# Edge tiles gathered once into a ring addressed through registers, in a graph-attention and mixture-of-experts kernel

## The reference

```python
xh = (x @ W).reshape(N, H, D)                    # H = 8 heads, D = 32
a_src = jnp.einsum('nhd,hd->nh', xh, att_src)
a_dst = jnp.einsum('nhd,hd->nh', xh, att_dst)
e = jax.nn.leaky_relu(a_src[src] + a_dst[dst], NEG_SLOPE)
m = jax.ops.segment_max(e, dst, num_segments=N)
e = jnp.exp(e - m[dst])
denom = jax.ops.segment_sum(e, dst, num_segments=N)
alpha = e / denom[dst]
msg = xh[src] * alpha[:, :, None]
out = jax.ops.segment_sum(msg, dst, num_segments=N).reshape(N, H * D) + bias
```

## Time and profile before

| what | value |
|---|---|
| time, median of 3 runs | 1908.13 us (1907.54 to 1909.66) |
| profiled execution | 1906.79 us, of which the span from first to last instruction is 1904.5 us |
| granted TensorE clock, mean | 0.952 |
| edge stage on DVE, first score to last add | 105.5 to 1200.0 us, 110 batches |
| busy over the whole span: PE, DVE, ACT, POOL | 89%, 74%, 58%, 64% |

### The profile page before, as it was taken

The page is one execution under the profiler, slowest core; times in us unless marked ns, Lnnn a source line. Parts: engine busy times, 40 slices in busy tenths (PEclk is TensorE's granted clock), DMA queues, the critical chain, the costliest instruction groups (busy, mean ns, idle before and its releaser), DMA issues. The chain is left out here.

```text
span 1904.5 us, 37710 instructions
## 1 busy us (share of the span) xinstructions
PE 1688.9 (89%) x10846; PEld 1183.9 (62%) x10846; DVE 1402.6 (74%) x3850; ACT 1106.3 (58%) x2386; POOL 1212.2 (64%) x1141
## 2 busy tenths in 40 slices
PE   6679889899898988989989798837999999999997
PEld 5445455455554645545555454625898898898995
DVE  6787778778687876887868778996666666666664
ACT  3556667667676666775767665773434434434343
POOL 1377777777777777777777777202566665665653
PEclk9889989989899998998999999977999999999999
DMA  8654555555555555545555453592333233333322
GB/s 282 215 147 123 143 167 145 137 154 143 167 145 134 156 142 167 146 132 155 145 167 145 127 139 104 218 351 77 48 52 52 47 53 51 48 53 49 49 44 32
DMA packets 124146, 240.41 MB, mean 126 GB/s; under 512 B 25064, under 2 KB 82996, under 8 KB 122772
## 3 DMA queue, kind: packets, MB, share of 16 engines
q0 software_dynamic: 62800, 147.76, 32.9%
q1 hardware_dynamic: 51816, 80.51, 12.9%
q10 hardware_dynamic: 9340, 9.73, 1.5%
HBM read 195.47 MB, written 43.30 MB: 125 GB/s over the span
## 5 line engine op out<-in xcount | busy, mean ns | idle before, releaser
L1142 POOL DMA_INDIRECT gather_ring<-node_table,src_slot x879 | 836.8, 952 | 270.6 <-issue 254.1
L1270 PE MATMUL bank<-gather_ring,onehot 128*128 128x264 f32 x1758 | 563.4, 403 | 51.1 <-DVE gather_ring L1194 50.3
L1236 PE MATMUL bank<-ones 128*128 128x512 bf16 x1787 | 558.0, 392 | 51.3 <-ACT gather_ring L1312 39.7
L1270 PEld LDWEIGHTS bank<-gather_ring,onehot 128*128 128x128 f32 x1758 | 293.8, 194 | 259.7 <-DVE gather_ring L1194 214.7
L1166 DVE TENSOR_TENSOR acc<-acc,bank 128x264 f32 x879 | 371.5, 423 | 14.1 <-PE bank L1270 13.1
L1194 DVE TENSOR_TENSOR gather_ring<-gather_ring,bank 128x256 f32<-128x256 f32 x879 | 363.3, 414 | 0.3 <-ACT bank L1311 0.3
L2164 POOL DMA_INDIRECT out_rows<-y,token_idx x105 | 202.7, 1930 | 218.1 <-DMA out_rows<-y,token_idx 155.7
L2133 ACT ACTIVATE hid<-bank,cols 128x256 f32<-128x256 f32 (+1 forms) x448 | 209.9, 550 | 148.5 <-PE bank L2074 145.6
L1236 PEld LDWEIGHTS bank<-ones 128*128 128x128 bf16 x1787 | 171.1, 100 | 199.5 <-issue 80.1
L2074 PE MATMUL bank<-xe,w_hi 128*128 128x256 f16 (+1 forms) x1792 | 285.3, 268 | 1.7 <-DVE xe L1996 1.5
L2091 PE MATMUL bank<-w,hid_hi 128*128 x1680 | 278.4, 273 | 0.0
(11 more groups left out here) (320 smaller groups left out, 1999.1 us busy)
## 6 DMA issues: line engine op xcount, KB each, us to landing
stage<-in_L_ffn_W SPq DMA_DIRECT2D x16, 1024.0 KB
dst_row<-dst_rows SPq DMA_DIRECT2D x110, 128.0 KB, 3.5
gather_ring<-node_table,src_slot POOLq DMA_INDIRECT x879
w_split<-w_out SPq DMA_DIRECT2D x32, 256.0 KB, 3.1
w<-w_split SPq DMA_DIRECT2D x8, 1024.0 KB, 9.8
node_table<-acc ACTq DMA_DIRECT2D x24, 264.0 KB
r_ring<-in_x_lanes SPq DMA_DIRECT2D x7, 896.0 KB, 8.1
xt<-in_x_lanes SPq DMA_DIRECT2D x24, 256.0 KB, 4.7
```

What stands on the lines that cost most here:

```text
L1142: e.indirect_dma_start(out=gather_ring[:, b % GB, j, :], out_offset=None, in_=node_table, in_offset=bass.IndirectOffsetOnAxis(ap=src_slot[ ...
L1236: e.matmul(to[:, :].rearrange("p (k n) -> p k n", k=2), halves[:, 0:P], halves.rearrange("p (a n) -> p a n", a=1).broadcast_to([P, 2, 2 * ...
L1270: e.matmul(bank[AGG[s % len(AGG)]][:, 0:ROW], onehot[:, b % OHB, j, :], gather_ring[:, b % GB, j, :], start=True, stop=True).then_inc(summ ...
```

## The change

Five edits that belong together:

- POOL gathers each **edge tile** once (832 indirect DMAs in 104 batches, the last tile padded) instead of each slot (879 in 110). `src_tile` takes the place of `src_slot`, and is made directly by loading `src_pad` and turning it, so that of the 14 indirect gathers of stage 1 seven are left.
- A slot no longer has a fixed place in `gather_ring`. Each slot's place (0 to 31) is worked out in stage 1 into `slot_table` and read into registers (`load_places`); the score and the message address the ring through them. `load_tiles` moves from before the score to after the second slot of the batch ahead; `load_places` stands after its sixth slot.
- Since rows are read by place, the score's first operation (128x64 for eight slots) becomes eight of 128x8.
- Since a tile may be read by two slots, a message can't overwrite its row: it goes to `message_ring` of 12 slots, from which PE reads; ACT writes the exponentials there. POOL waits for `messages`, up to a count read from `slot_table` (`SPANS_AT`, one register load for 8 batches).
- Which landing a batch of slots needs is known only on the chip. SP waits for it (`landed`, with counts in registers, loaded every other batch) and passes it on to DVE as `rows_landed`. The `onehot` ring shrinks from 3 to 2.

```diff
-        src_slot = early.take("src_slot", [P, SLOTS_UP], I32)
+        src_tile = early.take("src_tile", [P, ceil_div(ET, EB) * EB], I32)
...
+        MR = 12
+        message_ring = early.take("message_ring", [P, MR, ROW])
+        OHB = 2
...
+                    e.dma_start(raw_src[:, :, :], src_pad.rearrange("(c t) p -> t c p", t=P)).then_inc(src_loaded, 16)
...
+                e.tensor_copy(slot_table[SPANS_AT:SPANS_AT + 32, 0:SLOT_GROUPS * PER_GROUP],
+                              bank[7][SPANS_AT:SPANS_AT + 32, P:P + SLOT_GROUPS * PER_GROUP]).then_inc(slot_keys_made, 1)
+                for h in range(2):
+                    hs = slice(h * HALF_SLOTS, (h + 1) * HALF_SLOTS)
+                    vector_order.of(e.tensor_copy(slot_table[PLACES_AT:P, hs], bank[5 + h][PLACES_AT:P, 0:HALF_SLOTS]))
...
+                e.tensor_single_scalar(slot_table[PLACES_AT:LANDED_AT, :], slot_table[PLACES_AT:LANDED_AT, :], PLACES - 1,
+                                       ALU.bitwise_and).then_inc(slot_keys_made, 1)
...
+            if n == SRC_AT - 1:
+                e.wait_ge(src_loaded, 16)
+                e.tensor_copy(raw_src_f[:, :, :], raw_src[:, :, :]).then_inc(src_cast, 1)
...
+        def load_row_of(e, row, at, n, least, most):
+            _, values = nc.values_load_multi_w_load_instructions(
+                slot_table[row:row + 1, at:at + n], engines=[e.engine], min_val=least, max_val=most,
+                skip_runtime_bounds_check_because=IN_RANGE)
+            return values
...
         def pool_edges(e, batches):
-            for b in batches:
-                if b >= GB:
-                    e.wait_ge(summed, (b - GB + 1) * EB)
-                for j, s in enumerate(slots_in(b)):
+            for t in batches:
+                if t >= GB:
+                    if (t - GB) % SPANS_AT_ONCE == 0:
+                        at = t - GB
+                        spans = load_row_of(e, SPANS_AT, at, min(SPANS_AT_ONCE, TILE_BATCHES - GB - at), 1, USED)
+                    e.wait_ge(messages, spans[(t - GB) % SPANS_AT_ONCE])
+                    e.sem_inc(m_sems["passed"], 1)
+                for j, i in enumerate(tiles_of(t)):
                     e.indirect_dma_start(
-                        out=gather_ring[:, b % GB, j, :], out_offset=None, in_=node_table,
-                        in_offset=bass.IndirectOffsetOnAxis(ap=src_slot[:, s:s + 1], axis=0)
-                    ).then_inc(gathered[b % GB], 16)
+                        out=gather_ring[:, t % GB, j, :], out_offset=None, in_=node_table,
+                        in_offset=bass.IndirectOffsetOnAxis(ap=src_tile[:, i:i + 1], axis=0)
+                    ).then_inc(gathered[t % GB], 16)
...
             def score(b):
-                e.wait_ge(gathered[b % GB], 16 * (EB * (b // GB) + len(slots_in(b))))
+                e.wait_ge(rows_landed, GB * (b + 1))
...
-                vector_order.of(e.tensor_tensor(zbuf[:, 0, :, :], gather_ring[:, b % GB, :, D:ROW],
-                                                picked[:, b % 2, :, 0:HEADS], ALU.add))
+                for j in range(len(slots_in(b))):
+                    vector_order.of(e.tensor_tensor(zbuf[:, 0, j:j + 1, :], row_at(b, j)[:, :, D:ROW],
+                                                    picked[:, b % 2, j:j + 1, 0:HEADS], ALU.add))
...
+                if s >= MR:
+                    e.wait_ge(summed, s - MR + 1)
+                e.tensor_tensor(message_ring[:, s % MR, 0:D].rearrange("p (h d) -> p h d", d=DH),
+                                row_at(b, j)[:, :, 0:D].rearrange("p a (h d) -> p (a h) d", d=DH),
...
+                    if j == 1 and b + 1 < BATCHES:
+                        load_tiles(e, b + 1)
                     if j == EB // 2 - 1:
                         vector_weights_between(e, b)
+                    if j == EB - 3 and b + 1 < BATCHES:
+                        load_places(e, b + 1)
...
+            load_tiles(e, 0)
+            load_places(e, 0)
             sum_picks(0)
             for b in range(BATCHES):
-                load_tiles(e, b)
                 score(b)
...
+            def landed(b):
+                if b % 2 == 0 and b >= GB:
+                    values = load_row_of(e, LANDED_AT, b * GB, min(2, BATCHES - b) * GB, 16 * EB,
+                                         16 * EB * ceil_div(TILE_BATCHES, GB))
+                    landed_regs[b], landed_regs[b + 1] = values[0:GB], values[GB:]
+                for q in range(GB):
+                    if b >= GB:
+                        e.wait_ge(gathered[q], landed_regs[b][q])
+                    elif q <= b:
+                        e.wait_ge(gathered[q], 16 * EB)
+                    e.sem_inc(rows_landed, 1)
```

More of the change, by code:

```diff
@@ L186, in build_gnn_moe @@
         s1 = Region(early_b)
+        TILES_AT, SPANS_AT, PLACES_AT, LANDED_AT = 0, 32, 64, 96
+        PLACES = GB * EB
+        TILE_BATCHES = ceil_div(ET, EB)
+        assert PLACES & (PLACES - 1) == 0 and GB * BATCHES <= SLOTS_UP and SLOTS_UP // EB >= TILE_BATCHES
         iota_slot = s1.take("iota_slot", [P, SLOTS_UP])
         above = s1.take("above", [P, SLOTS_UP])
+        raw_src = s1.take("raw_src", [P, SLOT_GROUPS, P], I32)
+        raw_src_f = s1.take("raw_src_f", [P, SLOT_GROUPS, P])
         raw_idx = s1.take("raw_idx", [P, 4, P], I32)
@@ L236, in build_gnn_moe @@
         slot_base = s1w.take("slot_base", [P, SLOT_GROUPS])
+        PER_GROUP = P // EB
+        batch_end = s1w.take("batch_end", [P, PER_GROUP])
+        is_end = s1w.take("is_end", [P, PER_GROUP])
+        end_keys = s1w.take("end_keys", [P, SLOT_GROUPS, PER_GROUP])
+        last_batch = s1w.take("last_batch", [P, BATCHES], I32)
         pad_src = s1w.take("pad_src", [P, P], I32)
@@ L547, in vector_slot_step @@
                 e.tensor_scalar(above[:, :], iota_slot[:, :], key[:, 0:1], None, ALU.is_gt).then_inc(slots_counted, 1)
+                e.wait_ge(pool_const, BATCH_END)
+                vector_order.of(e.tensor_scalar(is_end[:, :], batch_end[:, :], part[:, 0:1], None, ALU.is_equal))
+                e.wait_ge(vector_order.sem, vector_order.n)
+                e.scalar_tensor_tensor(end_keys[:, :, :], key[:, :].rearrange("p (g a) -> p g a", a=1).broadcast_to(
+                    [P, SLOT_GROUPS, PER_GROUP]), 1.0, is_end[:, :].rearrange("p (a j) -> p a j", a=1).broadcast_to(
+                    [P, SLOT_GROUPS, PER_GROUP]), ALU.add, ALU.mult).then_inc(slots_counted, 1)
             elif 0 < c < SLOT_GROUPS:
-                e.wait_ge(slots_counted, c)
+                e.wait_ge(slots_counted, c + 1)
                 e.scalar_tensor_tensor(above[:, :], iota_slot[:, :], key[:, c:c + 1], above[:, :], ALU.is_gt, ALU.add
@@ new lines, in vector_slot_step @@
+            thresholds = slot_table[landed, 0:BATCHES * GB].rearrange("p (b q) -> p b q", q=GB)
+            if n == LISTS_AT + 5 + SLOT_GROUPS:
+                e.wait_ge(vector_order.sem, vector_order.n)
+                for q in range(GB):
+                    vector_order.of(e.tensor_single_scalar(thresholds[:, :, q], last_batch[landed, :], GB - q, ALU.add))
+                e.wait_ge(vector_order.sem, vector_order.n)
+                vector_order.of(e.tensor_single_scalar(thresholds, thresholds, 2, ALU.arith_shift_right))
@@ new lines, in vector_slot_step @@
+            g = n - LISTS_AT - 15
+            if 0 <= g < SLOT_GROUPS:
+                end = min((g + 1) * P, SLOTS)
+                e.wait_ge(slots_turned, g + 1)
+                e.tensor_single_scalar(neg_dst[:, g * P:end], bank[SLOT_TURN[g % 2]][:, 0:end - g * P], -1.0, ALU.mult
+                                       ).then_inc(slots_kept, 1)
+                e.wait_ge(slots_based, g + 1)
+                vector_order.of(e.tensor_scalar(row_up[:, :], raw_f[:, g % 2, :], 1.0, 0.0, ALU.add, ALU.max))
+                e.wait_ge(vector_order.sem, vector_order.n)
+                e.tensor_single_scalar(raw_row[:, g, :], row_up[:, :], float(P + 1), ALU.min
+                                       ).then_inc(rows_clamped, 1)
@@ L1295, in make_onehot, with ring_parts @@
                 one_where_zero(onehot[:, b % OHB, :, :], made, onehot_made)
+            def ring_parts(b):
+                first = min(EB, MR - b * EB % MR)
+                return [(0, first)] + [(first, EB - first)] * (first < EB)
             e.wait_ge(vector_const, MINUS_ONE_UP)
@@ L1311, in scalar_edges @@
                 e.activation(weights(b), zbuf[:, 1, :, :], ACT.Exp).then_inc(weighed, 1)
-                e.activation(gather_ring[:, b % GB, :, D:ROW], zbuf[:, 1, :, :], ACT.Exp).then_inc(weighed, 1)
+                if b:
+                    e.wait_ge(summed, (b + 1) * EB - MR)
+                for j, n in ring_parts(b):
+                    at = (b * EB + j) % MR
+                    made = e.activation(message_ring[:, at:at + n, D:ROW], zbuf[:, 1, j:j + n, :], ACT.Exp)
+                made.then_inc(weighed, 1)
                 if b + 2 < BATCHES:
@@ L1326, in load_row @@
```

(8 more changed lines are left out.)

148 lines of the change are left out of this document (83 added, 65 removed).

## The result

The changed kernel takes 1962.93 us (median of 4 runs, 1962.46 to 1967.12) against 1907.92 of the kernel before on the same chip: ratio 1.0297, 95% interval 1.0285 to 1.0309. The forecast was 1916 us with a range from 1874 to 1943. The sign is right, +55 us where +8 were forecast, and the time lies outside the range.

A forecast was written before the change was run, and what follows sets the result against it. POOL's issue rate bounds the edge stage before, DVE after: 110 x 1.23 = +135.3, less 144.8 of gather waits, +14 W1 blocks, +1.1 first loads, +3 stage 1 = +8.6 us; forecast 1916 us, range 1874 to 1943.

The forecast's parts named there:

- What bounds, and what POOL gives back: Edge stage: POOL's issue rate bounds before, DVE after; 47 fewer gathers free 59.1 us of POOL; DVE's 144.8 us wait goes.
- The rival in which POOL stays the bound: Edge stage: mid-batch loads covered and score pairs cheap, so DVE needs 8.75 us a batch; about 1855 us; chance 0.05.
- the one of SP's late landings: SP passes landings on late between stores and loads; at most some 0.5 us in each of eight batches; no chance given.
- Step 1, the joined score: DVE's score: eight 128x8 operations behind register instructions, 0.125 us a pair, replace one 128x64; +0.82 us a batch.
- The rival of cheap scores: DVE's score: register instruction and operation overlap, 0.08 us a pair; 35 us less in all, 1882 us; chance 0.22.
- Step 2, the register loads: DVE's batch: two mid-batch loads at 0.39 to 0.40 us each replace one at the turn (0.39); +0.41 us a batch.
- Step 3, the message's register instruction: DVE's messages: each one's own register instruction, 0.057 us, is hidden behind the running add, so it adds nothing.
- The rival of the lost cover: DVE's messages: the new register instruction lengthens each slot by 0.03 us, 26 us, 1942 us; chance 0.17 together with a dearer pair.
- The W1 blocks: Eight batches where DVE waits for picks behind a block's load: saved gather wait partly returns, mean 1.8 us each, +14 us.
- Start and stage 1: First two loads ahead of the first picks and score, +1.1 us; DVE's small work in stage 1, +3 us (0 to +6).

The follow-up runs named there:

- The fastest version: Changed kernel, both tables in words on partition 0, places loaded right behind the sum of the picks, tiles behind mid-batch W1 work: 1901.7 us, ratio 0.9957.
- four kernels above: Changed kernel, both loads at the turn: 2352.1 us; kernel before with two turn loads: 2187.2; second from partition 64: 1906.9; score in eight without registers: 1907.9.

## Why the prediction was wrong, step by step

- **What bounds, and what POOL gives back:** right. DVE is the bound, POOL's wait for the messages is 103.4 us (forecast +40; it is larger by about what DVE became slower), the gathers are as short as before, and DVE's 144.8 us of waiting are gone. The rival in which POOL stays the bound falls by this, and the one of SP's late landings too: DVE waits for no landing of rows in this trace.
- **Step 1, the joined score, +0.82 us:** right. 1.08 - 0.26 = 0.82 in the batch shown, 0.85 in the mean over the batches. The pair that I took at 0.125 us averages 0.129. The rival of cheap scores falls: 0.08 us is what they cost without their register instructions.
- **Step 2, the register loads, +0.41 us: this is the step that failed.** Its first half holds: the turn gives back 0.39. Its second half, "two loads at 0.39 to 0.40 each", was 0.69 each. The messages' idle time is 132.9 us, and the load also takes the 0.08 us by which a message otherwise starts before the add has ended: 132.9 + 218 x 0.08 = 150 us over 109 batches, 1.38 us against my 0.80, or 64 us more in all. Of these the change of partition makes 218 x 0.22 = 48 us, shown by the loads of one partition (46 to 48 us of time came back). Another 14 us are 31 loads of over 0.95 us. The pricing of the gap itself was nearly sound: with both loads in one partition it is (81.0 + 17) / 109 = 0.90 us, of which 0.09 are 26 loads of over 0.72 us. That this kernel takes 1915.5 us, and my forecast was 1916, is luck all the same: its loads cost 11 us more than I put, and the W1 blocks 10 less. I had taken 0.597 us from a row of a kernel that only ever loads from one partition, and had not seen this as a condition of the row.
- **Step 3, the message's register instruction:** hidden, as said, wherever no load stands (0.67 us a slot). Behind a load it is not: the message starts 0.15 us after the load's end, where in the kernel before with its load moved, whose messages have none, it is 0.05. This tenth of a microsecond, twice a batch, did not show in the sum, because a load in the middle of a batch without it costs 0.29 us and not my 0.40. The two errors cancelled by luck. The rival of the lost cover falls.
- **The W1 blocks, +14 us: too much.** DVE waits 21.1 us for those picks against 19.0, and from a batch's first dependent score to its first message the mean over 110 batches went from 2.155 to 2.161 us, 0.7 us in all. A slower DVE, for which the block's load has landed by the time DVE comes, can explain only a part. The kernel with both tables in words on partition 0 takes 9.98 us a batch, about the pace that I had forecast, and there the wait is 23.8 us and the same mean 2.194, 4 us in all. The fastest version, at 9.85, waits 33.9. So the term was too large at its own pace, and it grows when DVE gets faster; no run tests it alone, and why it was too large stays open.
- **Start and stage 1, +4.1 us:** right. First gather at 87.9 us (forecast 87.5), first score at 110.49, +4.9.

The sum: between first score and last add I forecast 135.3 - 144.8 + 14 = +4.5 us; with 64 more for the loads and 13 less for W1 it is +55.5, and measured is (1258.15 - 110.49) - (1199.61 - 105.55) = +53.6. The last add of the changed kernel, in order of time:

```profile
1258.15 0.43 DVE L1240 TENSOR_TENSOR acc<-acc,bank 128x264 f32 x1 [0.21 <-PE bank L1358]
```

What stays open: of the 31 long loads 24 overlap a load or a DMA issue of SP, but 41 others overlap one and are not long, and of the 880 loads at the turn (those of the kernel before and of four kernels above) one was over 0.95 us. What makes them long was not settled, and with them 14 of the 64 us stay unexplained. Nor was it tried what in the change of partition costs the 0.2 us. Other pairs of partitions stand only once in a trace, where an engine goes from a flag on partition 0 to its own row of the table, so these are hints. SP's first load from partition 96 takes 0.743 us where its later ones take 0.528 (the same 0.2 more), POOL's first from partition 32 takes 0.597 against 0.565, hardly more than the first load of the kernel before on DVE, which changes no partition (0.615 against 0.597).

## What to carry to other kernels

A duration read from a trace holds for the conditions of that row: before multiplying it by new instructions, ask in what they differ (here another partition of the same table; in bytes instead of words it is three times as much). Where DVE loads registers from more than one table, keep the tables in one partition, as words, and put the loads right behind the longest operation that the loop has. Measure more than one number of values to a load: two words took longer here than four. When the page names a releaser that was done long ago for a new gap, look at what the engine's own sequencer does there: 122 us stood here under PE's name and belonged to register loads. And a term that came out right in the sum may hide two errors, as the register instruction behind a load did.

## What the runs showed of the hardware that I had not expected

- A register load of eight words takes 0.597 us on DVE if the load before it on that engine read the same partition, and 0.81 us if it read another one (0 and 64, in either direction). A load of four words pays the same 0.22 us, 120 us after the other one.
- On DVE two words take 0.529 us, four 0.346, eight 0.597, sixteen 1.125 (one load; 1.32 with a change of partition). Eight values of one byte take 1.836 us, two 0.514.
- Operations of 128x8 start 0.081 us apart on DVE in the mean, and 0.129 apart with a register instruction ahead of each.
- On one chip the kernel before took 2185.5 us and not 1908, 15% more. In the traces of the variants that ran there DVE stood still for up to 13.5 us at a time, with a granted TensorE clock of 0.87 to 0.91 over the whole execution (0.95 for the kernel before and 0.96 for the changed one elsewhere); the median durations of its messages, adds and register loads were the same as elsewhere. The cause stays open.
